# Large attentions: probabilities turned in 32x32 squares and through DRAM scratch, context sums two slots later

## Chip, cores and metric

One Trainium2 chip, one core. The metric is device time in microseconds; the kernel before takes 2303.13 us (median of 3 runs, 2302.65 to 2303.64).

## What is computed

Two decoder layers' worth of cross attention over 8 batches: a first attention with 16 heads of 32 and its MLP, then two attentions with 16 heads of 128 (`a` = 0 and 1), each with one extra key and value row, and a last MLP. The change concerns the two large attentions. Cut to what matters, with h the normalized rows (8 x 112 of them, 512 wide) and ctx the context (8 x 375 keys, 512 wide):

```
for a in (0, 1):
    h = layer_norm(x)
    q = (h @ wq + bq).reshape(8, 112, 16, 128)
    k = concat(ctx @ wk + bk, bias_k)          # 376 keys, 16 heads of 128
    v = concat(ctx @ wv + bv, bias_v)
    weights = softmax(einsum('bqhk,bthk->bhqt', q, k) / sqrt(128))
    x = x + einsum('bhqt,bthk->bqhk', weights, v).reshape(8, 112, 2048) @ wo + bo
h = gelu(layer_norm(x) @ w_fc1 + b_fc1) @ w_fc2 + b_fc2
return x + h
```

## The kernel before

Each product is made of three fp32r matmuls of halves (hi x hi, lo x hi, hi x lo; lines 1766, 1767, 1768), so every operand is split into a hi half (ScalarE) and a lo half (VectorE or GpSimd).

An attention runs over 4 groups of 4 heads, in each over 8 batches b = 0 to 7 (`Place`; two batches are a pair, four a quad, `parity` = b % 2 picks the buffer), in each over 4 tiles t = 0 to 3, one head each. I call one pass of the loop over t in `one_batch` a slot. In a slot TensorE makes the keys of the tile three slots on (`key`, 12 matmuls of 376 columns into ps_k), one column of context sums (`context_sum`, 9 matmuls of 448 columns) of the batch before, turns the probabilities of the next tile (`turn`, line 1963: three transposes against an identity into ps_t), and makes the scores of the tile two slots on (`scores`, 3 matmuls of 376 columns). The value projection is taken out of the sum over keys: a context sum is the context weighted by the probabilities of all four heads (moving operand `pt`, 4 x 112 columns), four of them (d = 0 to 3) per batch; after each quad `head_output` multiplies the sums with the value weights, 12 matmuls of 448 columns for each of 4 heads. `chunks` and `heads` say which sums and outputs lie in which slot: a slot of b = 1 or 5 has outputs in t = 0 and 1 (not in group 0 for b = 1) and two sums in t = 2 and 3.

The softmax of a tile: VectorE takes the maximum (1538), ScalarE the exponential with its sum (1141), VectorE the reciprocal, the extra key's probability and the scaling (1423, 1547, 1426). After the turn ScalarE writes the hi half of the turned tile (1117) and VectorE the lo half (1554). ScalarE and VectorE also split keys (1110, 1532) and sums (1124, 1560). All engines run instructions in program order, and each of the functions named exists once per engine, in the same order of slots. All DMAs are issued by SyncE in program order on one queue; an issue whose semaphore is not there yet holds all that follow. The context comes from DRAM scratch, as halves by feature (`cs`, two buffers) and by key (`ckd`, two buffers of 2 x 768 KB). The value weights of the next group are loaded late in b = 1 (`place.loads`), and their halves made there: hi on ScalarE (899), lo on GpSimd (806).

At the end of an attention (`epilogue`) come the last sums and outputs, then the output projection (`project`), 7 row tiles of 12 matmuls of 512 columns for each of 4 groups; its first two row tiles (`EARLY_TILES`) take operands that lie ready early, the third waits for all output evictions (z_ev), and the halves of its operands are made by ScalarE 1212 and VectorE 1636.

## Time and profile before

| | |
|---|---|
| time, median of 3 runs | 2303.13 us |
| profiled execution: span from first to last instruction | 2301.3 us |
| first large attention, about | 604 to 1220 us of the span |
| second large attention, about | 1390 to 2066 us |
| TensorE busy | 2273.7 us (99%) |
| VectorE / ScalarE / GpSimd busy | 1339.3 / 1122.5 / 359.4 us |
| granted TensorE clock | 0.999 of full speed |
| DMA | 376.25 MB, 163 GB/s on average |

For the profiled execution the profile gives the span; a run's time holds a little more, what lies before the first and after the last instruction (2303.13 - 2301.3 = 1.8 us by the median). In rows with durations, an instruction's start and how long it was in the engine stand first; matmuls are pipelined, so that what one costs is the distance between two starts and not its length. Busy shares are averages over the span.

### The profile page before, as it was taken

The page shows a single profiled execution, that of the slowest core. Times are in us where ns is not written, and L with a number is a line of the kernel's source. Part 1 is how long each engine was busy: PE and PEld are TensorE (multiplying, and loading weights), DVE is VectorE, ACT ScalarE, POOL GpSimd, SP SyncE. Part 2 cuts the span into 40 slices and gives each one's busy share as a digit, 9 for nine tenths or more (in the row PEclk, how much of TensorE's full clock was granted, in tenths as well). Part 3 has the DMA queues.
Part 4 walks back from the last instruction along what each step waited for, and adds up shares of the span by engine and source line. Part 5 has one row for each costly group of instructions (what it writes and reads, how often), then busy time and mean ns, then how long its engine had stood idle before and what let it go on. Part 6 is the DMA issues. An engine that isn't in the chain of part 4 may idle for free.

```text
span 2301.3 us, 37087 instructions
## 1 busy us (share of the span) xinstructions
PE 2273.7 (99%) x13091; PEld 2061.8 (90%) x13091; DVE 1339.3 (58%) x3102; ACT 1122.5 (49%) x2468; POOL 359.4 (16%) x727
## 2 busy tenths in 40 slices
PE   7999999999999999999999999999999999999999
PEld 6777788889999999999998899999999999998887
DVE  6877774524655655665664526565565565564743
ACT  5777753344444445454453434445445445453421
POOL 2111065320000101001002210001001001012421
PEclk9999999999999999999999999999999999999999
DMA  5422135574554755745744554555556556454110
GB/s 196 139 90 104 62 112 195 170 245 134 191 191 151 237 181 166 232 170 181 230 142 146 210 167 147 205 192 184 193 191 198 179 191 213 164 167 132 54 55 33
DMA packets 255224, 376.25 MB, mean 163 GB/s; under 512 B 90302, under 2 KB 205906, under 8 KB 255042
## 3 DMA queue, kind: packets, MB, share of 16 engines
q1 hardware_dynamic: 255042, 373.87, 48.3%
q8 instruction: 108, 1.77, 0.3%
q14 instruction: 74, 0.61, 0.1%
HBM read 315.77 MB, written 58.05 MB: 162 GB/s over the span
## 4 chain that ended last, share of the span: by engine, by line
PE 94%; DVE 3%; ACT 1%; issue 1%; DMA 0%; SPq 0%; DVEq 0%; ACTq 0%
PE ps_k L1766 10%; PE ps_k L1767 10%; PE ps_k L1768 10%; PE ps_o L1766 9%; PE ps_o L1768 9%; PE ps_o L1767 9%; PE ps_v L1766 6%; PE ps_v L1768 6%; PE ps_v L1767 6%; PE ps_s L1766 4%; PE ps_s L1768 4%; PE ps_s L1767 4%; PE ps_t L1963 3%; PE ps_t L1901 2%; PE ps_s L1888 1%
## 5 line engine op out<-in xcount | busy, mean ns | idle before, releaser
L1766 PE MATMUL ps_k<-cs_hi,w_a_hi 128*128 128x376 f32 x1132 | 383.0, 338 | 0.0
L1767 PE MATMUL ps_k<-cs_lo,w_a_hi 128*128 128x376 f32 x1132 | 378.6, 334 | 0.0
L1768 PE MATMUL ps_k<-cs_hi,w_a_lo 128*128 128x376 f32 x1132 | 377.6, 334 | 0.0
L1141 ACT ACTIVATE prob<-ps_s,row_columns 112x376 f32<-112x376 f32 x256 | 147.2, 575 | 304.0 <-DVE row_columns L1538 304.0
L851 POOL CAST k_hi<-xk_hi 128x1 fp32r<-128x1 f32 x256 | 47.0, 184 | 1226.6 <-PE ps_s L1768 1226.6
L1766 PEld LDWEIGHTS ps_k<-cs_hi,w_a_hi 128*128 128x128 f32 x1132 | 213.1, 188 | 1.3 <-issue 0.3
L1767 PEld LDWEIGHTS ps_k<-cs_lo,w_a_hi 128*128 128x128 f32 x1132 | 213.2, 188 | 0.5
L1768 PEld LDWEIGHTS ps_k<-cs_hi,w_a_lo 128*128 128x128 f32 x1132 | 213.2, 188 | 0.0
L1532 DVE SCALAR_TENSOR_TENSOR k_lo<-ps_k,col_b,k_hi 128x375 fp32r<-128x375 f32 x252 | 152.8, 606 | 72.5 <-ACT k_hi L1110 66.9
L1110 ACT ACTIVATE k_hi<-ps_k,col_b 128x375 fp32r<-128x375 f32 x252 | 143.7, 570 | 82.7 <-PE ps_k L1768 81.7
L1423 DVE RECIPROCAL row_columns<-row_columns 112x1 f32<-112x1 f32 x384 | 62.6, 163 | 195.1 <-ACT prob L1141 187.4
L806 POOL TENSOR_TENSOR w_b_lo<-w_raw_b,w_b_hi 128x512 fp32r<-128x512 f32 x80 | 108.0, 1379 | 387.3 <-ACT w_b_hi L899 387.2
L1426 DVE TENSOR_SCALAR prob<-prob,row_columns 112x375 f32<-112x375 f32 x384 | 162.7, 424 | 4.5
L1560 DVE TENSOR_TENSOR sums_lo<-ps_o,sums_hi 128x448 fp32r<-128x448 f32 x128 | 80.0, 625 | 131.2 <-ACT sums_hi L1124 131.1
L1538 DVE TENSOR_REDUCE row_columns<-ps_s 112x1 f32<-112x376 f32 x256 | 138.4, 540 | 8.3 <-PE ps_s L1768 8.1
L1768 PE MATMUL ps_o<-pt_hi,ckd_lo 128*128 128x448 f32 (+1 forms) x384 | 140.6, 366 | 0.0
L1766 PE MATMUL ps_o<-pt_hi,ckd_hi 128*128 128x448 f32 (+1 forms) x384 | 140.5, 366 | 0.0
L1767 PE MATMUL ps_o<-pt_lo,ckd_hi 128*128 128x448 f32 (+1 forms) x384 | 140.0, 365 | 0.0
L1124 ACT ACTIVATE sums_hi<-ps_o 128x448 fp32r<-128x448 f32 x128 | 69.8, 545 | 141.4 <-PE ps_o L1768 141.3
L1768 PE MATMUL ps_v<-pt_hi,ckd_lo 128*128 128x448 f32 x378 | 138.4, 366 | 0.0
L1767 PE MATMUL ps_v<-pt_lo,ckd_hi 128*128 128x448 f32 x378 | 137.6, 364 | 0.0
L1766 PE MATMUL ps_v<-pt_hi,ckd_hi 128*128 128x448 f32 x378 | 137.4, 364 | 0.0
(283 smaller groups left out, 5749.5 us busy)
## 6 DMA issues: line engine op xcount, KB each, us to landing
ckd_hi<-context_by_key_halves SPq DMA_DIRECT2D x64, 768.0 KB, 4.5
ckd_lo<-context_by_key_halves SPq DMA_DIRECT2D x64, 768.0 KB, 6.4
cs_hi<-context_halves SPq DMA_DIRECT2D x64, 752.0 KB, 6.2
cs_lo<-context_halves SPq DMA_DIRECT2D x64, 752.0 KB, 7.9
w_raw_b<-in_blocks_b SPq DMA_DIRECT2D x104, 256.0 KB, 4.1
w_raw_a<-in_blocks_a SPq DMA_DIRECT2D x104, 256.0 KB, 4.3
q<-q_scratch SPq DMA_DIRECT2D x72, 224.0 KB, 6.3
extra<-extra_probability SPq DMA_DIRECT2D x16, 896.0 KB, 5.1
```

Source lines behind the costliest of these rows:

```text
L806: pool.tensor_tensor(w[slot][1][:, :, part], w_raw[slot][:, :, part], w[slot][0][:, :, part], ALU.subtract).then_inc(w_lo[slot], 1)
L1110: act.activation(k[t % 2][0][:, 0:LK], key_bank(place, t)[:, 0:LK], ACT.Identity, bias=col_b[:, ds(place.column((C_BK0, C_BK1), t), 1)]).t ...
L1124: act.activation(sums[0][:, d, place.quarter * HALF:(place.quarter + 1) * HALF], ps_c[d % 2][:, 0:HALF], ACT.Identity).then_inc(c_hi, 1)
L1141: act.activation(prob[buf][0:LQ, 0:KW], ps_s[buf][0:LQ, 0:KW], ACT.Exp, bias=max_neg[0:LQ, buf:buf + 1], accum_out=prob_sum[0:LQ, buf:buf ...
L1426: dve.tensor_scalar(p[0:LQ, 0:LK], p[0:LQ, 0:LK], prob_rcp[0:LQ, col:col + 1], None, ALU.mult).then_inc(s_norm, 1)
L1532: dve.scalar_tensor_tensor(out=k[t % 2][1][:, 0:LK], in0=key_bank(place, t)[:, 0:LK], scalar=col_b[:, ds(place.column((C_BK0, C_BK1), t), 1)],
L1538: dve.tensor_reduce(max_neg[0:LQ, t % 2:t % 2 + 1], ps_s[t % 2][0:LQ, 0:KW], AX_X, ALU.max, negate=True).then_inc(s_max, 1)
L1560: dve.tensor_tensor(sums[1][:, d, cols], ps_c[d % 2][:, 0:HALF], sums[0][:, d, cols], ALU.subtract).then_inc(c_lo, 1)
L1766: pe.matmul(out, w_h, m_h, start=first, stop=False)
L1767: pe.matmul(out, w_h, m_l, start=False, stop=False)
L1768: return pe.matmul(out, w_l, m_h, start=False, stop=last)
L1963: last = pe.transpose(ps_t[buf][0:n, i * LQ:(i + 1) * LQ], prob[buf][0:LQ, k0:k0 + n], ident[0:LQ, 0:LQ])
```

## The change

The probabilities are no longer turned by TensorE. VectorE transposes each tile in 32x32 squares into one buffer, `blocks` (128 x 1536 for the 4 heads of a batch); SyncE stores `blocks` to DRAM scratch and loads it back with 4 DMAs of 32 partitions each, which puts the squares where the turned matrix has them, into the lo half of `pt`; ScalarE makes the hi half of a whole batch in one pass (`turned_hi`, 1536 columns) and GpSimd the lo half in three (`turned_lo`, 512 columns each). The context sums of a batch move two slots later. Queries are padded from 112 to 128 rows per batch in scratch and in the scores (so the query parts are 448 and 448 columns instead of 512 and 384); keys alternate between two PSUM banks; `ckd` becomes one buffer in four parts, each loaded when the sum that used it is done; outputs of a quad lie in t = 2 and 3; weights of the next group are split in t = 0 and 1 of b = 2 and loaded in t = 1 of it. In the epilogue the last two sums of b = 6 and the first two row tiles of the projection lie ahead of the last batch's sums, and the four last outputs are made in two halves.

```diff
-        self.loads = isinstance(self.b, int) and self.b == 1 and not self.head
+        self.loads = isinstance(self.b, int) and self.b == att.loading and (group > 0 or not att.layer and not self.head)
...
-        return {2: (0, 1), 3: (2, 3)}.get(t, ()) if self.att.layer and self.loads else ()
+        return {0: (0, 1), 1: (2, 3)}.get(t, ()) if self.att.layer and self.loads else ()
...
         def chunks(place, t):
 
-            if place.before() is None:
+            last = place.before()
+            if t >= 2:
+                return () if last is None or outputs_here(place) else ((last, t - 2),)
+            if last is None or last.before() is None:
                 return ()
-            if place.final:
-                return {0: (0,), 1: (1, 2), 2: (3,)}.get(t, ())
-            if place.quarter != 1 or place.head:
-                return (t,)
-            return {2: (0, 1), 3: (2, 3)}.get(t, ())
+            return ((last.before(), 2 * t), (last.before(), 2 * t + 1)) if outputs_here(last) else ((last.before(), t + 2),)
...
+                def store_blocks(place):
+                    sp.wait_ge(block_turn, unit_1(place, NT))
+                    sp.sem_inc(sp_waited, 1)
+                    sp.dma_start(turned_scr[place.parity], blocks[:]).then_inc(blocks_out, 16)
+
+                def load_turned(place):
+                    sp.wait_ge(blocks_out, 16 * place.visit + 16)
+                    wait(sp, c_mm, NT * (place.visit - 1))
+                    sp.sem_inc(sp_waited, 1)
+                    src = turned_scr[place.parity].rearrange("(i a) (s f) -> s a i f", i=BANDS, s=4)
+                    for s in range(4):
...
+                        sp.dma_start(dst, src[s]).then_inc(turned_in[place.parity], 16)
...
+                    for t in range(NT):
+                        if t == 0 and place.after(2):
+                            sp.wait_ge(k_mm, place.tile + NT)
...
+                            load_halves(place.after(2))
...
+                        if t == 1 and place.after(2):
+                            load_q(place.after(2))
+                        if t == 2:
+                            store_extra(place)
+                            store_blocks(place)
+                        if t == 3:
+                            load_turned(place)
...
+                        for summed, d in chunks(place, t):
+                            load_by_key(summed.next(), d)
+                        if t == 1 and place.loads:
+                            load_block(1, place.block_b + 1)
+                            load_block(0, place.block_a + 1)
...
+                def turned_lo(place):
+                    pool.wait_ge(t_hi, place.visit + 1)
+                    for i in range(3):
...
+                        pool.tensor_tensor(lo, lo.bitcast(F32), hi, ALU.subtract).then_inc(t_lo, 1)
...
+                        if t == 1 and place.before():
+                            turned_lo(place.before())
                         split_lo(1, place.block_b, place.split_own(t))
...
+                def turned_hi(place):
+                    act.wait_ge(turned_in[place.parity], 64 * place.pairs + 64)
+                    act.activation(pt[place.parity][0][:], pt[place.parity][1][:].bitcast(F32),
+                                   ACT.Identity).then_inc(t_hi, 1)
...
                         if place.key(t + 2):
                             exp(*place.key(t + 2))
+                        if t == 0 and place.before():
+                            turned_hi(place.before())
...
+                    outputs_hi(a, 0, (z_half, a + 1))
                     for t in range(NT):
                         extra_term(place, t)
-                    outputs_hi(a, 0, (z_mm, NT * place.quads + NT))
...
+                    dve.wait_ge(s_norm, place.unit + t + 1)
+                    if t == 0:
+                        wait(dve, blocks_out, 16 * place.visit)
+                    dve.transpose(blocks[:].rearrange("p (s j t e) -> p t j s e", s=4, j=3, t=NT)[:, t],
+                                  prob[buf][:, 0:BLOCKS * SQUARE].rearrange("p (j s e) -> p j s e", j=3, s=4)).then_inc(block_turn, 1)
...
+                    for c in range(len(OUT_CHUNKS)):
+                        outputs_lo(a, 0, c)
                     for t in range(NT):
                         output(place, t)
-                    for c in range(len(OUT_CHUNKS)):
-                        outputs_lo(a, 0, c)
...
                     if d == 0:
-                        pe.wait_ge(t_lo, NT * place.visit + NT)
-                        pe.wait_ge(ck_in[place.parity], 32 * place.pairs + 32)
+                        pe.wait_ge(t_lo, 3 * place.visit + 3)
+                    pe.wait_ge(ck_in[d], 16 * place.visit + 16)
...
                 def epilogue(place):
-                    first_final_sum(place)
-                    for d in range(1, DT):
+                    for d in (2, 3):
+                        context_sum(place.before(), d)
...
+                    for r in range(EARLY_TILES):
+                        project_row(1, 0, 0, 5 * RT + 4 * RT * a, r, early)
+                    for d in range(DT):
                         context_sum(place, d)
-                    for t in range(NT):
-                        head_output(place, t)
+                    for part in ((0, 2), (2, DT)):
+                        for t in range(NT):
+                            head_output(place, t, part)
```

How the order of instructions moves, at three places. A number behind a name is the buffer's.

ScalarE, the end of one batch and the first slot of the next in an ordinary stretch; before:

```order
L1110 ACTIVATE k1_hi<-ps_k,col_b 128x375 [waits k_mm,s_mm]
L1124 ACTIVATE sums_hi<-ps_v 128x448 [waits c_mm]
L1117 ACTIVATE pt0_hi<-ps_t1 128x3x112 [waits t_mm]
L1141 ACTIVATE prob0,row_columns<-ps_s0,row_columns 112x376 [waits t_mm,s_max]
L1110 ACTIVATE k0_hi<-ps_k,col_b 128x375 [waits k_mm,s_mm]
```

and now:

```order
L1178 ACTIVATE k1_hi<-ps_t0,col_b 128x375 [waits k_mm,s_mm]
L1190 ACTIVATE sums_hi<-ps_v 128x448 [waits c_mm]
L1207 ACTIVATE prob0,row_columns<-ps_s0,row_columns 128x376 [waits block_turn,s_max]
L1183 ACTIVATE pt0_hi<-pt0_lo 128x1536 [waits turned_in0]
L1178 ACTIVATE k0_hi<-ps_k,col_b 128x375 [waits k_mm,s_mm]
L1190 ACTIVATE sums_hi<-ps_o1 128x448 [waits c_mm]
```

The hi half of a tile in each slot has become one pass of 1536 columns per batch, behind the exponential (L1207) of slot 0.

GpSimd and SyncE, slots 0 to 2 of b = 2 in groups 1 to 3 (before, the weights w_b lay in b = 1 and GpSimd had no `pt`); now on GpSimd:

```order
L859 TENSOR_TENSOR w_b_lo<-w_raw_b,w_b_hi 128x4x128 [waits w_hi_b] x2
L904 COPY k0_hi<-xk_hi 128x1 [waits s_mm]
L905 COPY k0_lo<-xk_lo 128x1
L912 TENSOR_TENSOR pt1_lo<-pt1_lo,pt1_hi 128x512 [waits t_hi]
L912 TENSOR_TENSOR pt1_lo<-pt1_lo,pt1_hi 128x512 x2
L859 TENSOR_TENSOR w_b_lo<-w_raw_b,w_b_hi 128x4x128 [waits w_hi_b] x2
```

and on SyncE:

```order
L612 DMA cs0_hi<-context_halves 128x1504 [waits k_mm]
L612 DMA cs0_lo<-context_halves 128x1504
L618 DMA ckd<-context_by_key_halves 128x768 [waits c_mm] x2
L658 DMA q<-q_scratch 128x4x128 [waits s_mm]
L618 DMA ckd<-context_by_key_halves 128x768 [waits c_mm] x2
L577 DMA w_raw_b<-in_blocks_b 128x4x128 [waits w_lo_b] x4
L577 DMA w_raw_a<-in_blocks_a 128x4x128 [waits w_lo_a] x4
L702 DMA extra_probability<-extra_p 128x4 [waits extra_ev]
L716 DMA turned_probabilities<-blocks 128x1536 [waits block_turn]
L618 DMA ckd<-context_by_key_halves 128x768 [waits c_mm]
L726 DMA pt0_lo<-turned_probabilities 32x4x384 [waits blocks_out,c_mm]
```

The batch's turned probabilities stand behind two weight passes on GpSimd, and the store of this batch's squares behind eight weight loads on SyncE, two of which wait for the weight passes that stand behind the probabilities.

ScalarE at the end of an attention; before:

```order
L1133 ACTIVATE extra<-extra,col_b,extra_delta 128x448 [waits extra_in,z_ev]
L1133 ACTIVATE extra<-extra,col_b,extra_delta 128x448 [waits z_ev] x3
L1212 ACTIVATE act_t_hi<-cs0_hi 128x4x80 [waits z_mm,p_in0]
L1212 ACTIVATE act_t_hi<-cs0_lo 128x3x4x112 [waits z_mm,p_in1]
L1212 ACTIVATE act_t_hi<-cs1_hi 128x2x4x112 [waits z_mm,p_in2]
```

and now:

```order
L1183 ACTIVATE pt1_hi<-pt1_lo 128x1536 [waits turned_in1]
L1190 ACTIVATE sums_hi<-ps_v 128x448 [waits c_mm]
L1190 ACTIVATE sums_hi<-ps_o1 128x448 [waits c_mm]
L1190 ACTIVATE sums_hi<-ps_v 128x448 [waits c_mm]
L1190 ACTIVATE sums_hi<-ps_o1 128x448 [waits c_mm]
L1273 ACTIVATE act_t_hi<-cs0_hi 128x4x80 [waits z_half,p_in0]
L1273 ACTIVATE act_t_hi<-cs0_lo 128x3x4x112 [waits z_half,p_in1]
L1273 ACTIVATE act_t_hi<-cs1_hi 128x2x4x112 [waits z_half,p_in2]
L1199 ACTIVATE extra<-extra,col_b,extra_delta 128x448 [waits extra_in,z_ev]
L1199 ACTIVATE extra<-extra,col_b,extra_delta 128x448 [waits z_ev] x3
```

The terms of the last four outputs (L1199, before L1133) have moved behind the three operand passes of the projection.

## Rows read from the trace of the kernel before

**Rows 1.** The page: busy us (share of the span) and instructions of each engine.

```profile
PE 2273.7 (99%) x13091; PEld 2061.8 (90%) x13091; DVE 1339.3 (58%) x3102; ACT 1122.5 (49%) x2468; POOL 359.4 (16%) x727
```

**Rows 2.** Timeline of TensorE, one slot: start us, length us, engine, line, operation.

```profile
1019.89 0.36 PE L1768 MATMUL ps_o<-pt_hi,ckd_lo 119*128 119x448 f32 x1
1020.09 0.46 PE L1963 MATMUL ps_t<-ident,prob 112*128 112x112 f32 x3
1020.32 0.41 PE L1766 MATMUL ps_s<-k_hi,q 128*112 128x376 f32 x1
...
1020.91 0.34 PE L1766 MATMUL ps_k<-cs_hi,w_a_hi 128*128 128x376 f32 x1
...
1022.97 0.36 PE L1766 MATMUL ps_v<-pt_hi,ckd_hi 128*128 128x448 f32 x1
...
1024.79 0.46 PE L1963 MATMUL ps_t<-ident,prob 112*128 112x112 f32 x3
```

**Rows 3.** The chain that ended last, this slot: start, share of the chain in us.

```profile
1020.25 0.30 PE ps_t L1963 x3
```

**Rows 4.** Timelines of ScalarE and VectorE in the same slot.

```profile
1022.40 0.58 ACT L1141 ACTIVATE prob<-ps_s,row_columns 112x376 f32<-112x376 f32 x1 [1.22 <-DVE row_columns L1538]
1022.96 0.62 ACT L899 ACTIVATE w_a_hi<-w_raw_a 128x512 fp32r<-128x512 f32 x1
...
1020.87 0.62 DVE L1560 TENSOR_TENSOR sums_lo<-ps_o,sums_hi 128x448 fp32r<-128x448 f32 x1 [0.61 <-ACT sums_hi L1124]
1021.41 0.50 DVE L1554 TENSOR_TENSOR pt_lo<-ps_t,pt_hi 128x336 fp32r<-128x336 f32 x1
1021.82 0.54 DVE L1538 TENSOR_REDUCE row_columns<-ps_s 112x1 f32<-112x376 f32 x1
...
1023.42 0.41 DVE L1426 TENSOR_SCALAR prob<-prob,row_columns 112x375 f32<-112x375 f32 x1
```

**Rows 5.** Groups by line and shape: ScalarE passes of SBUF; count, busy us, mean ns.

```profile
L1212 ACT ACTIVATE act_t_hi<-cs_lo 128x1344 fp32r<-128x1344 f32 x8 | 10.6, 1327 | 24.3 <-PE ps_v L1768 24.3
L1212 ACT ACTIVATE act_t_hi<-cs_hi 128x896 fp32r<-128x896 f32 x8 | 7.6, 952 | 8.8 <-PE ps_o L1768 8.8
```

**Rows 6.** Timelines of GpSimd and VectorE: half passes inside an attention, and behind it.

```profile
913.26 2.58 POOL L806 TENSOR_TENSOR w_b_lo<-w_raw_b,w_b_hi 128x512 fp32r<-128x512 f32 x2 [8.65 <-ACT w_b_hi L899]
...
1223.95 5.92 POOL L806 TENSOR_TENSOR w_b_lo<-w_raw_b,w_b_hi 128x512 fp32r<-128x512 f32 x4 [31.97 <-ACT w_b_hi L899]
...
1224.02 2.19 DVE L1636 TENSOR_TENSOR act_t_lo<-cs_hi,act_t_hi 128x896 fp32r<-128x896 f32 x1
```

**Rows 7.** Timeline of SyncE's DMA issues, weight loads in b = 1.

```profile
917.80 5.12 SPq L541 DMA_DIRECT2D w_raw_b<-in_blocks_b  x4
922.97 3.24 SPq L541 DMA_DIRECT2D w_raw_a<-in_blocks_a  x4
```

**Rows 8.** DMA issues: count, KB each, median us from issue to landing.

```profile
cs_lo<-context_halves SPq DMA_DIRECT2D x64, 752.0 KB, 7.9
...
w_raw_a<-in_blocks_a SPq DMA_DIRECT2D x104, 256.0 KB, 4.3
...
context_by_key_halves<-ckd_hi SPq DMA_DIRECT2D x8, 768.0 KB, 3.3
context_by_key_halves<-ckd_lo SPq DMA_DIRECT2D x8, 768.0 KB, 5.4
```

**Rows 9.** Busy time of the engines in one batch: us; clock, DMA share, GB/s last.

```profile
1000.00:1018.77 18.77, 18.77 (x110) 18.06 (x109) 11.32 (x29) 8.93 (x22) 1.21 (x8) 1.00 0.49 179
```

**Rows 10.** Groups by line and shape: what the last outputs of an attention take.

```profile
L1133 ACT ACTIVATE extra<-extra,col_b,extra_delta 128x448 f32<-128x448 f32 x64 | 75.8, 1185 | 8.2 <-DVE o L1570 8.2
...
L1570 DVE TENSOR_TENSOR o<-ps_s,extra 128x448 f32<-128x448 f32 x4 | 2.5, 626 | 7.3 <-PE ps_s L1768 7.3
...
L1636 DVE TENSOR_TENSOR act_t_lo<-cs_lo,act_t_hi 128x1344 fp32r<-128x1344 f32 x8 | 12.5, 1557 | 4.8 <-ACT act_t_hi L1212 4.8
...
L1636 DVE TENSOR_TENSOR act_t_lo<-cs_hi,act_t_hi 128x896 fp32r<-128x896 f32 x8 | 10.9, 1368 | 1.4 <-ACT act_t_hi L1212 1.3
```

370 lines of the change are left out of this document (162 added, 208 removed).

## The prediction

> **What bounds the kernel now.** I read the page first: TensorE is busy for 2273.7 of 2301.3 us [rows 1], so time leaves only where its stream gets shorter, and comes back wherever it has to wait. Then the timeline of TensorE over one slot of a large attention [rows 2]. From the transposes at 1020.09 to those at 1024.79 a slot takes 4.70 us: 12 key matmuls from 1020.91 to 1022.97 (2.06 us), 9 matmuls of a context sum from there to 1024.79 (1.82 us), and 0.82 us for transposes and scores. Nothing waits. The reader should see that the distance between starts counts, not the lengths. A batch is 4 such slots, 18.77 us [rows 9], with TensorE busy throughout and VectorE for 11.3 us, ScalarE for 8.9 us.
>
> **What is saved.** Transposes to first score matmul take 0.23 us, and the first score matmul behind them runs longer than the others; the chain of waits puts 0.30 us of the slot down to the three transposes [rows 3]. There are 2 x 4 x 8 x 4 = 256 of these groups: 256 x 0.30 = 76.8 us. A slot becomes 4.40 us. Padding the stationary queries to 128 leaves the count of moved columns as it is, and 448 + 448 query columns are as many as 512 + 384: nothing. Scores, maximum, exponential and scaling run on 128 partitions instead of 112 at the same columns: nothing. VectorE's lo half of a tile (0.41 us from its start to the next instruction's [rows 4]) makes room for the squares. I have no row for a transpose on VectorE; the scaling of 375 columns takes 0.41 us and a two-input pass of 896 columns 1.37 us, so 0.59 us by columns for 384 [rows 4, 10]. At either end VectorE has about 12 us of work in a batch of 17.6 us and stays hidden.
>
> **The wait that replaces them.** Where does the first sum of a batch stand, and when is its lo half there? Call S the start of the scores in slot 0. Their position today is the transposes' 1020.09, since those are gone. Behind S TensorE runs 0.51 us of scores, slot 1 (4.40) and the keys of slot 2 (2.06), and at S + 6.97 it wants the sum d = 0 of the batch before, which waits for all three lo passes.
>
> The lo passes hang on that slot's exponential. VectorE starts the sum's lo half at 1020.87 (S + 0.78) and the next instruction at 1021.41 (S + 1.32); that is now the maximum. ScalarE's exponential starts 0.58 us behind the maximum's start and the next ScalarE instruction 0.56 us behind that [rows 4]: `turned_hi` starts at S + 2.46. Its 1536 columns: 896 take 0.95 us and 1344 take 1.33 [rows 5], so 1.49 us; done at S + 3.95. GpSimd takes 1.29 us for a pass of 512 columns inside an attention [rows 6], three take 3.87; with 0.1 us of handing over, S + 7.95. So TensorE waits **1.0 us in an ordinary batch**, against 1.2 us that its four slots save. No semaphore in this chain depends on how early the DMAs land.
>
> Per attention the 20 places where it applies, and one in the epilogue:
>
> - 15 ordinary batches (group 0: b = 2, 3, 4, 7; later b = 0, 3, 4, 7 except the last batch): 15 x 1.0 = 15.0 us. In b = 1 and 5 of later groups (5 alone in group 0) outputs stand in these slots, and in b = 6, with two sums in slots 0 and 1, there is room (S + 8.8): no wait.
> - b = 1 of group 0: slots 0 and 1 hold no sums, so TensorE arrives at S + 5.14 and the chain, with no sum ahead of the maximum, ends near S + 7.3: 2.2 us.
> - b = 2 of groups 1 to 3: two weight passes stand ahead of `turned_lo` on GpSimd. ScalarE makes their hi halves behind `turned_hi`, they end at S + 7.1, the extra key's copies at S + 7.4, the lo passes at S + 11.3; with two sums in slot 1 TensorE arrives at S + 8.8. 3 x 2.5 = 7.5 us.
> - b = 3 behind it. On SyncE the loads of w_b wait for the weights' second pair of passes, which GpSimd does behind the lo passes, to S + 13.9. Today too these loads hold SyncE, 5.12 us, and the four of w_a behind them 0.81 us each [rows 7], but nothing urgent follows. Now the store of b = 2's squares does, ready at S + 10: it is issued near S + 17.8, lands at S + 22 (3.3 us [rows 8] and the loads ahead of it), and VectorE, which must not write `blocks` before, stands at the first square of b = 3 from S + 16.7 on, 5.3 us. Behind it are the keys' lo halves and the next maximum. TensorE first waits 1.0 us for a key; then the exponential ahead of `turned_hi` is late, and at the first sum TensorE waits 3.6 us, of which 1.0 is counted above. 3 x 3.6 = 10.8 us.
> - The last batch has no keys left to cover with: TensorE arrives at S + 2.9 for halves that come at S + 8.0, 5.1 us. Its own halves are asked for after 4 sums (7.3 us) and 2 projection tiles (24 matmuls, 5.5 us) and are about 1.0 us late. 6.1 us.
> - The last four outputs: the projection's third row tile waits for all their evictions. Their terms now stand behind three hi passes on ScalarE (320, 1344 and 896 columns, 2.6 us), their evictions behind three lo passes on VectorE (1.56 and 1.37 us and a short one), and as there is one `term` buffer, each takes 1.19 + 0.63 us in turn [rows 5, 10]. From the moment half the output matmuls are done: lo passes to 4.9, then four evictions to about 11.5 us, while TensorE is through its second half (24 matmuls of 0.20) at 4.9. The two row tiles that cover this today lie earlier now: 6.6 us.
> - Between the second and third output of a quad only the scores are left as cover (0.51 us for an eviction of 0.63 and its handovers): about 0.3 us x 7 = 2.1 us. At the start, slots without sums (2.57 us) run ahead of VectorE's 3.1 us per tile: 1.0 us.
>
> Together 15.0 + 2.2 + 7.5 + 10.8 + 6.1 + 6.6 + 3.1 = 51.3, twice 102.6 us. Change: 102.6 - 76.8 = +25.8. The profiled execution's span is 2301.3 us, so the changed one's 2327; the median of the runs lies 1.8 us above the span, so **2329 us**.
>
> **GpSimd's passes, both ways.** Inside an attention a pass takes 1.29 us; behind it, beside VectorE passes of two SBUF operands, four take 5.92 us, 1.48 each, and VectorE's 896-column pass 2.19 instead of 1.37 us [rows 6, 10]. I take 1.29, since that row lies between the same VectorE instructions; 1.48 is the other end: 3 x 0.19 us at 42 places, +24 us, 2353 us. The Trainium skill (GPSIMD Engine Reference, section Specifications) says that GpSimd and VectorE share the SBUF interface, and contend when VectorE works in a two-port mode or on two SBUF inputs; by that rule the scaling of the probabilities would slow the passes too. The trace agrees behind the attention (1.48 us) and shows none of it inside (1.29 us).
>
> **Scratch.** A batch moves 179 GB/s x 18.77 us = 3.36 MB at 0.49 of the engines' time [rows 9]; the store and loads of 786 KB each raise that to about 0.73. Not the bound, as long as the round trip is in time: squares ready at S1 + 3.9 (S1 in slot 1), store 3.3 us, 1.6 us for four issues, 4.3 us to land [rows 8]: S1 + 13.1, and `turned_hi` could start at S1 + 16.6. The other end, 5.4 and 7.9 us, gives S1 + 18.8, 2.2 us late.
>
> **The rivals.**
>
> *The halves are in time (faster).* One mechanism: if the chain from scores to the last lo pass is shorter than I have it, every one of the 42 waits shrinks. From 0.6 us less the change is even (42 x 0.6 = 25); at 1.0 us less the ordinary batches wait for nothing: 2329 - 42 = 2287, and if VectorE also catches up before b = 3's sum, half of 21.6 us more, 2276 us. For it: three parts of the chain are extrapolated (the 1536 columns, GpSimd on contiguous tiles, the maximum right behind the sum). Against it: each is from a row next to its place, and 0.6 us is 8% of 7.95.
>
> *Scratch comes last (slower still).* If store and loads take the upper rows, `turned_hi` is late by 2.2 us at the 42 places: +92, 2421 us. The point where it starts is 3.5 us more than I have. For it: the loads go to 32 partitions each, which no row shows, and share one queue with 1.5 MB of context. Against: 3.5 us of room, and the context is issued either well before the store or behind the loads.
>
> **Numbers.** Forecast 0.68, in time 0.20, scratch last 0.12. About 0.2% (4.6 us) is what a measurement of this kernel can tell from no change. Of the forecast 0.04 falls within it and 0.03 below (the waits at b = 3 and the end partly hidden), of the first rival 0.03 within: faster 0.20, same 0.07, slower 0.73. The forecast's own range is 2303 to 2356 (GpSimd's upper row and a little); to hold 8 in 10 the range goes down to 2278 and leaves out most of the scratch rival: 2278 to 2356.
>
> **What would show it.** The list of waits of TensorE should show first matmuls of context sums waiting for GpSimd's pt_lo about 42 times: about 77 us in all, 1.0 us in most, 2.5 and 3.6 in b = 2 and 3 of groups 1 to 3, 5.1 in the last batch; and about 6.6 us each before two projection tiles, for VectorE's output. GpSimd passes 1.29 us, `turned_hi` 1.49 us. SyncE should hold a store for some 8 us in each b = 2. A slot without waits should be 4.40 us. If these waits are absent, or TensorE waits for ckd or for other DMAs instead, the prediction is wrong in that step; if `turned_hi` waits for its DMA in ordinary batches, the second rival is right.

## The result, and the profile after

| | before | after |
|---|---|---|
| median of the runs, us | 2303.4 (2302.7 to 2304.1, 4 runs) | 2409.0 (2407.3 to 2412.1, 4 runs) |
| ratio to before | | 1.046, 95% interval 1.0445 to 1.0474 |
| span of the profiled execution, us | 2301.3 | 2409.9 |
| mean granted clock of TensorE | 0.999 | 0.979 |

The changed kernel is 4.6% slower. The prediction was 2329 us, within 2278 to 2356: the sign was right, the gain of the shorter slots was more than eaten by waits and by TensorE at half clock, and the size was wrong by 80 us.

The page of after, busy time of each engine, answers to [rows 1]:

```profile
PE 2258.8 (94%) x12323; PEld 2027.3 (84%) x12323; DVE 1384.3 (57%) x3102; ACT 1116.7 (46%) x2276; POOL 609.1 (25%) x919
```

TensorE issues 768 instructions less, the three transposes of 256 groups, and is yet busy for only 15 us less. It stands still for 151.1 us, against 27.6 before. What it waits for, from the list of waits of TensorE in after (engine, what it writes and line, releaser: us in total, times, longest; "issue" is a wait for nothing that the profile shows):

```profile
PE ps_v L1820 <- POOL pt_lo L912: 63.0, 40, 5.1
PE ps_o L1820 <- DVE o L1632: 20.5, 30, 6.3
PE ps_v L1820 <- issue: 18.5, 2, 9.5
PE ps_s L1820 <- DVE k_lo L1594: 16.0, 10, 3.8
...
PE ps_s L1820 <- DVE q L1481: 4.5, 8, 0.9
```

The first two rows are near what was predicted (77 us for all waits for the lo halves, 17 for the outputs), the keys' 16.0 us were forecast as 6, the queries' not at all. The third row is two waits only, one in each attention, of about 9 us: the first sum, forecast among the lo halves at 2.2 us each. The groups by line and shape in after, for the new operations:

```profile
L912 POOL TENSOR_TENSOR pt_lo<-pt_lo,pt_hi 128x512 fp32r<-128x512 f32 x192 | 245.3, 1307 | 227.2 <-ACT pt_hi L1183 227.2
...
L1616 DVE STREAM_TRANSPOSE blocks<-prob 128x384 f32<-128x384 f32 x256 | 148.1, 579 | 68.4 <-DMA turned_probabilities<-blocks 60.3
...
L1183 ACT ACTIVATE pt_hi<-pt_lo 128x1536 fp32r<-128x1536 f32 x64 | 94.5, 1477 | 13.3 <-DMA pt_lo<-turned_probabilities 13.3
```

Each duration is within 0.02 us of the prediction's (1.29, 0.59, 1.49). And the DMA issues of after (count, KB each, median us to landing), which answer to [rows 8]:

```profile
turned_probabilities<-blocks SPq DMA_DIRECT2D x64, 768.0 KB, 3.8
pt_lo<-turned_probabilities SPq DMA_DIRECT2D x256, 192.0 KB, 4.0
```

**Where the span's 108.6 us come from.** I took the starts of TensorE's instructions through both attentions and compared each distance with its distance where nothing waits. Distances above that behind a wait sum to 140.8 us in after, 3.7 in before: +137.1. A 448-column matmul over 28-column runs takes 0.206 us from start to start instead of 0.2025: 3072 of them, +10.8. The share of the clock that was not granted while TensorE was busy sums to 37.6 us in after, none in before. With the -76.8 that were forecast for the transposes: 137.1 + 10.8 + 37.6 - 76.8 = 108.7. Each term is good to a few us only (it depends on which distances count as a wait), so that the sum comes out within 0.1 is luck. This is where the time lies; it does not say yet what each part would give back.

**The clock.** The windows of after, right behind the first sum's wait and over the 50 us around it (us, busy us and instructions of PE, PEld, DVE, ACT, POOL, then granted clock, DMA share, GB/s):

```profile
575.14:579.30 4.16, 4.16 (x12) 3.77 (x13) 1.77 (x4) 0.43 (x1) 0.27 (x2) 0.50 0.48 193
...
550.00:600.00 50.00, 37.63 (x190) 34.88 (x189) 27.09 (x61) 17.99 (x37) 10.34 (x24) 0.90 0.66 207
```

The timeline of TensorE in the same stretch shows what half the clock (1.2 of 2.4 GHz) does:

```profile
575.14 0.71 PE L1820 MATMUL ps_v<-pt_hi,ckd 128*128 128x448 f32 x1 [9.53 <-issue]
575.65 0.57 PE L1821 MATMUL ps_v<-pt_lo,ckd 128*128 128x448 f32 x1
576.02 0.57 PE L1822 MATMUL ps_v<-pt_hi,ckd 128*128 128x448 f32 x1
...
582.12 0.37 PE L1822 MATMUL ps_o<-pt_hi,ckd 128*128 128x448 f32 x1
582.33 0.37 PE L1820 MATMUL ps_o<-pt_hi,ckd 128*128 128x448 f32 x1
```

A matmul starts every 0.37 us instead of every 0.21. In after the granted clock was 0.50 from 569.5 us, within the wait, to 579.7. In before it stayed at 1.00 through both attentions, and TensorE hardly stood still there (3.7 us).

**The first sum.** Why did it wait 9.7 us and not 2.2? SyncE's DMA issues in b = 0 of group 0, in after:

```profile
553.04 0.36 SPq L716 DMA_DIRECT2D turned_probabilities<-blocks  x1
556.83 0.32 SPq L640 DMA_DIRECT2D q_scratch<-o  x1
562.21 0.55 SPq L577 DMA_DIRECT2D w_raw_b<-in_blocks_b  x1
562.87 1.97 SPq L726 DMA_DIRECT2D pt_lo<-turned_probabilities  x4
```

and ScalarE and GpSimd behind it:

```profile
569.77 1.48 ACT L1183 ACTIVATE pt_hi<-pt_lo 128x1536 fp32r<-128x1536 f32 x1 [5.91 <-DMA pt_lo<-turned_probabilities]
...
571.33 1.26 POOL L912 TENSOR_TENSOR pt_lo<-pt_lo,pt_hi 128x512 fp32r<-128x512 f32 x1 [10.95 <-ACT pt_hi L1183]
```

The squares were in scratch at 558.00 (there VectorE's next one starts), but SyncE issued their loads at 562.87, behind the weights of the last query piece, which wait until VectorE has split the weights they overwrite. In slots 0 and 1 of b = 1 TensorE has no sums to do, so the late issue is passed on whole.

### The profile page after: what moved, and what is told of

Its sections match the earlier page's. It is cut to its first block, busy times and chain, and to the rows that moved or that the text cites. A ratio compares the mean times of both kernels' runs of the same rounds, so it can differ in the third digit from the quotient of the medians.

```text
span 2409.9 us, 36258 instructions
## 1 busy us (share of the span) xinstructions
PE 2258.8 (94%) x12323; PEld 2027.3 (84%) x12323; DVE 1384.3 (57%) x3102; ACT 1116.7 (46%) x2276; POOL 609.1 (25%) x919
## 3 DMA queue, kind: packets, MB, share of 16 engines
q8 instruction: 101, 1.65, 0.3%
## 4 chain that ended last, share of the span: by engine, by line
PE 67%; DVE 10%; POOL 6%; ACT 6%; issue 6%; DMA 4%; SPq 1%; DVEq 0%; ACTq 0%; POOLq 0%
PE ps_o L1820 7%; PE ps_o L1822 6%; PE ps_o L1821 6%; PE ps_v L1820 5%; PE ps_v L1822 5%; PE ps_v L1821 5%; POOL pt_lo L912 5%; PE ps_k L1820 5%; PE ps_k L1821 4%; PE ps_k L1822 4%; PE ps_s L1820 3%; PE ps_s L1822 3%; PE ps_s L1821 3%; DMA turned_probabilities<-blocks 3%; PE ps_t L1821 2%
## 5 line engine op out<-in xcount | busy, mean ns | idle before, releaser
L1207 ACT ACTIVATE prob<-ps_s,row_columns 128x376 f32<-128x376 f32 x256 | 147.1, 575 | 378.0 <-DVE row_columns L1600 377.9
L912 POOL TENSOR_TENSOR pt_lo<-pt_lo,pt_hi 128x512 fp32r<-128x512 f32 x192 | 245.3, 1307 | 227.2 <-ACT pt_hi L1183 227.2
L1820 PE MATMUL ps_v<-pt_hi,ckd 128*128 128x448 f32 (+1 forms) x384 | 155.1, 404 | 81.4 <-POOL pt_lo L912 63.0
L1820 PE MATMUL ps_k<-cs_hi,w_a_hi 128*128 128x376 f32 x636 | 219.5, 345 | 0.0
L1821 PE MATMUL ps_k<-cs_lo,w_a_hi 128*128 128x376 f32 x636 | 214.7, 338 | 0.0
L1822 PE MATMUL ps_k<-cs_hi,w_a_lo 128*128 128x376 f32 x636 | 213.2, 335 | 0.0
L1488 DVE TENSOR_SCALAR prob<-prob,row_columns 128x375 f32<-128x375 f32 (+1 forms) x384 | 177.4, 462 | 4.5
L1821 PE MATMUL ps_t<-cs_lo,w_a_hi 128*128 128x376 f32 x512 | 170.8, 334 | 0.0
L1822 PE MATMUL ps_t<-cs_hi,w_a_lo 128*128 128x376 f32 x512 | 170.4, 333 | 0.0
L1820 PE MATMUL ps_t<-cs_hi,w_a_hi 128*128 128x376 f32 x512 | 170.1, 332 | 0.0
L1822 PE MATMUL ps_v<-pt_hi,ckd 128*128 128x448 f32 (+1 forms) x384 | 150.4, 392 | 0.0
L1822 PE MATMUL ps_o<-pt_hi,ckd 128*128 128x448 f32 (+1 forms) x384 | 142.8, 372 | 0.0
L1820 PE MATMUL ps_o<-pt_hi,ckd 128*128 128x448 f32 (+1 forms) x384 | 142.5, 371 | 0.0
```

The costliest lines, as they stand in the source:

```text
L912: pool.tensor_tensor(lo, lo.bitcast(F32), hi, ALU.subtract).then_inc(t_lo, 1)
L1207: act.activation(prob[buf][:, 0:KW], ps_s[buf][:, 0:KW], ACT.Exp, bias=max_neg[:, buf:buf + 1], accum_out=prob_sum[:, buf:buf + 1]).then_i ...
L1488: dve.tensor_scalar(p[rows, 0:LK], p[rows, 0:LK], prob_rcp[rows, col:col + 1], None, ALU.mult).then_inc(s_norm, 1)
L1820: pe.matmul(out, w_h, m_h, start=first, stop=False)
L1821: pe.matmul(out, w_h, m_l, start=False, stop=False)
L1822: return pe.matmul(out, w_l, m_h, start=False, stop=last)
```

## The experiments

Times are medians, to be read against after's 2409.0 us; each kernel had its own runs of before beside it (2302.8 to 2303.5 us). The first four take one suspect each: ScalarE's order, the weights in b = 2, SyncE's order at the start, and the clock.

### ScalarE's hi pass ahead of the exponential

```diff
+                        if t == 0 and place.before():
+                            turned_hi(place.before())
                         if place.key(t + 2):
                             exp(*place.key(t + 2))
-                        if t == 0 and place.before():
-                            turned_hi(place.before())
```

Expected: 

> ScalarE's hi pass over the landed tiles stands ahead of the exponential of its slot instead of behind it. Theory (the late lo halves come from ScalarE's order): turned_hi starts about 1.6 us earlier (S + 0.8 instead of S + 2.46), the last lo pass ends near S + 6.3 instead of S + 7.95, the ordinary wait of 0.8 us is gone, those of 1.2 to 2.3 us lose about 1.5 and the one of the last batch goes from 5.3 to about 3.7; together about 20 us per attention: 2409 -> 2365 us (2355 to 2375). Rival (GpSimd or the scratch transfers set the moment anyway): the waits stay, the exponential is only later: 2405 to 2415 us.

Measured: 2400.1 us (2397.2 to 2405.9), ratio 1.0416 (1.0399 to 1.0434). The waits for the lo halves fell from 63.0 to 29.2 us, as the theory has it, and the ordinary wait is gone. But those for VectorE grew: keys 16.0 to 24.5, queries 4.5 to 14.6, and the first sum 18.5 to 21.0. Where the squares land late (b = 0 of group 0, b = 3), the hi pass now holds the exponential behind it, and with it VectorE. And `turned_hi`, now earlier, waited for its transfer in 32 batches (61.6 us in all) instead of 6 (13.3 us). The order is a cause of the late halves, and changing it alone is worth 9 us, not 44: neither range holds.

### Weights later in b = 2

```diff
-                        if t == 1 and place.loads:
+                        if t == 3 and place.loads:
                             load_block(1, place.block_b + 1)
                             load_block(0, place.block_a + 1)
...
-                        split_lo(1, place.block_b, place.split_own(t))
+                        split_lo(1, place.block_b, place.split_own(t - 1))
```

(the second load goes with the condition of the first)

Expected: 

> In b = 2 of groups 1 to 3 SyncE's loads of the next weights move from slot 1 to the end of slot 3 and GpSimd's two pairs of weight passes one slot later, behind turned_lo. Theory (SyncE is held by its own weight loads, GpSimd by the weight passes): the waits of b = 2 (2.3 us) fall to the ordinary 0.8, those of b = 3 (2.1 for the keys, 3.3 for the lo halves) to 0 and 0.8, and the stretches at half clock behind them go (some 2 to 3 us each place): 6 places x 8 us: 2409 -> 2360 us (2350 to 2372). Rival (the waits of b = 2 and 3 come from the scratch traffic beside the loads): they stay, 2405 to 2412 us.

Measured: 2386.4 us (2385.9 to 2388.5), ratio 1.0363 (1.0347 to 1.0378). That is 23 us, half of what was expected. The waits of b = 2 and 3 went to 0.8 us or nothing; two new ones came. VectorE and SyncE's issues in b = 3 of this run:

```profile
787.57 0.32 SPq L716 DMA_DIRECT2D turned_probabilities<-blocks  x1
...
796.42 2.12 SPq L726 DMA_DIRECT2D pt_lo<-turned_probabilities  x4
...
796.42 0.58 DVE L1616 STREAM_TRANSPOSE blocks<-prob 128x384 f32<-128x384 f32 x1 [4.41 <-DMA turned_probabilities<-blocks]
```

The store took 8.8 us to land, behind the weights and the context in the one queue; VectorE may not write `blocks` before, stood for 4.4 us, and the sum of the next batch waited 3.3 us. In the six places like it the store took 7.6 to 9.3 us. The other new wait: GpSimd and VectorE in slot 1 of b = 2.

```profile
764.99 2.54 POOL L859 TENSOR_TENSOR w_b_lo<-w_raw_b,w_b_hi 128x512 fp32r<-128x512 f32 x2
...
767.86 2.95 POOL L859 TENSOR_TENSOR w_b_lo<-w_raw_b,w_b_hi 128x512 fp32r<-128x512 f32 x2
...
766.47 1.28 DVE L1488 TENSOR_SCALAR prob<-prob,row_columns 128x375 f32<-128x375 f32 x1
...
768.28 1.39 DVE L1481 TENSOR_TENSOR q<-q 128x512 fp32r<-128x512 f32 x1
```

Scaling took 1.28 instead of 0.41 us, the queries' lo half 1.39 instead of 0.65, each beside a GpSimd pass, and TensorE waited 1.95 us for the queries.

### The squares' loads ahead of the late query piece

```diff
+                        if t == 3:
+                            load_turned(place)
                         if query_piece(place, t):
                             last_query(query, a, skip, query_piece(place, t))
...
-                        if t == 3:
-                            load_turned(place)
-                            if place.quarter == 3:
-                                load_extra(place)
+                        if t == 3 and place.quarter == 3:
+                            load_extra(place)
```

Expected: 

> SyncE issues the loads of the turned squares ahead of the late query piece in slot 3 (in b = 0 of group 0 alone that is a difference of order). Theory (in b = 0 SyncE is held by the last query piece and the weights behind it): the loads are issued 4.9 us earlier (558.0 instead of 562.9), the wait at the first sum falls from 9.7 and 9.1 us to about 4 us each, with less time at half clock behind: 2409 -> 2397 us (2393 to 2400). Rival (the landing of the loads, not their issue, is late): within 2 us of 2409.

Measured: 2393.2 us (2390.1 to 2401.8), ratio 1.0397 (1.0376 to 1.0417): -15.8. The timelines of SyncE and TensorE:

```profile
552.51 0.36 SPq L716 DMA_DIRECT2D turned_probabilities<-blocks  x1
557.50 1.75 SPq L726 DMA_DIRECT2D pt_lo<-turned_probabilities  x4
...
568.95 0.51 PE L1820 MATMUL ps_v<-pt_hi,ckd 128*128 128x448 f32 x1 [3.83 <-issue]
```

The loads go out as soon as the store has landed, and 3.8 us of wait are left. Settled: this place, once in each attention, is worth 16 us, nearly a fifth of the miss. By the starts of TensorE, 12 of them lie at the place itself (5.9 and 6.1 us). Why 3.8 us are left and not the 2.2 that were forecast, no run takes apart.

### TensorE kept busy behind the waits

```diff
+            def busy(n):
+                for _ in range(n):
+                    pe.transpose(ps_t[1][:, 0:P], ident[:], ident[:])
...
                     if d == 0:
+                        busy(fillers(place))
                         pe.wait_ge(t_lo, 3 * place.visit + 3)
```

(and the same ahead of the scores of b = 3, slot 0, and of the third row tile)

Expected: 

> No wait is touched; ahead of TensorE's long waits stand transposes of the identity into an unread bank (100, 22, 34, 54, 18 and 70 of them), in length a little under the wait. Theory (the clock that falls behind a wait costs some 38 us by itself): the waits end at the same times, the granted clock stays at full behind them, and 2409 -> 2378 us (2370 to 2390). Rival (the clock falls anyway or the 38 us are not the clock's): within 3 us of 2409; and where the filler at half clock runs past the end of a wait, above 2409.

Measured: 2404.9 us (2401.9 to 2407.1), ratio 1.044 (1.0425 to 1.0456), at a mean clock of 0.997. That is 4 us, between the theory and the rival. The identity's transposes took 0.108 us each, more than I had counted, and ran past the waits. So once more, shorter:

Expected: 

> As the first filler run, whose transposes took 0.108 us each and so ended up to 1.2 us behind the waits that they should fill: now 83, 17, 27, 44, 15 and 54 of them, 9.0 to 1.6 us. Theory (TensorE at half clock behind the waits has a price, but a part of it is taken from the next wait): the first run saved 7 us with some 13 us of overruns, so 2409 -> 2390 us (2384 to 2397). Rival (the half clock costs nothing in the end, since the next wait takes it all): 2404 to 2411. Rival (all 38 us are the clock's): 2371 to 2377.

Measured: 2400.0 us (2397.2 to 2400.6), ratio 1.0414 (1.0396 to 1.0431), clock 0.997. Again between the ranges. Half clock is left in four stretches, behind waits of 1.8 to 2.7 us, and 6.7 us are lost in them while TensorE is busy, against 37.6 in after; the first of them:

```profile
961.10:964.50 3.40, 3.40 (x13) 3.40 (x12) 2.60 (x8) 1.56 (x4) 0.30 (x2) 0.50 1.03 224
```

So some 31 us of clock were given back, and 9 us of time came of it. Where did the others go? In the first sum TensorE's stretch is shorter by 2 us and stays so. In b = 2 to 3 it is not. VectorE, then TensorE, of the shorter filler, and the same two instructions of after:

```profile
779.76 0.58 DVE L1616 STREAM_TRANSPOSE blocks<-prob 128x384 f32<-128x384 f32 x1 [8.37 <-DMA turned_probabilities<-blocks]
...
776.95 1.80 PE L1999 MATMUL ps_t<-ident 128*128 128x128 f32 x15
...
780.88 0.44 PE L1820 MATMUL ps_s<-k_hi,q 128*128 128x376 f32 x1 [2.12 <-DVE k_lo L1594]
```

```profile
780.66 0.58 DVE L1616 STREAM_TRANSPOSE blocks<-prob 128x384 f32<-128x384 f32 x1 [6.59 <-DMA turned_probabilities<-blocks]
...
781.79 0.44 PE L1820 MATMUL ps_s<-k_hi,q 128*128 128x376 f32 x1 [1.96 <-DVE k_lo L1594]
```

TensorE reaches the place at 776.95 instead of 779.83 (781.79 less its wait of 1.96), 2.9 us earlier, but starts only 0.9 us earlier: VectorE stands 8.4 us for the store instead of 6.6. The store's landing sets the moment. By the distances between starts, waits (79 us) and fillers (716 of 0.108 us, 77) through both attentions are about 157 us against 140 of waits in after: some 17 us of what the clock gave back went into them. So half clock is a price where nothing else is late behind it (2 us at each first sum), and is taken out of the next wait where a transfer is.

### Contiguous columns

This kernel leaves out the reordering of the turned columns: it multiplies others of them, and what it returns is not the attention.

```diff
-            by_band = pt[place.parity][part][:].rearrange("p (i j t e) -> p j i t e", i=BANDS, j=3, t=NT)
-            return by_band[0:KEY_TILES[i][1], i, :, :, 0:BAND]
+            return pt[place.parity][part][0:KEY_TILES[i][1], i * HALF:(i + 1) * HALF]
...
-            return tile.rearrange("p (g t e) -> p t g e", g=4 * BANDS, t=NT)[:, t]
+            return tile[:, t * HALF:(t + 1) * HALF]
```

Expected: 

> The sums and the head outputs read 448 columns in one run instead of 28-column runs with 4 (or 96) skipped between them; the number of matmuls, columns and waits is the same, which columns are multiplied is not (the sums and outputs are of other rows). Theory: a matmul takes 0.2033 us from start to start instead of 0.207, 3072 of them: -11 us, 2409 -> 2398 us (2395 to 2401). Rival (the pitch does not hang on the runs): 2409 within 2 us.

Measured: 2402.5 us (2401.9 to 2404.8), ratio 1.0434 (1.0419 to 1.045): -6.5 us. The starts of one sum in slots without a wait, of this run and of after:

```profile
637.29 0.36 PE L1819 MATMUL ps_o<-pt_hi,ckd 128*128 128x448 f32 x1
...
638.91 0.37 PE L1821 MATMUL ps_o<-pt_hi,ckd 119*128 119x448 f32 x1
```

```profile
637.78 0.37 PE L1820 MATMUL ps_o<-pt_hi,ckd 128*128 128x448 f32 x1
...
639.43 0.37 PE L1822 MATMUL ps_o<-pt_hi,ckd 119*128 119x448 f32 x1
```

Eight steps take 1.62 us here and 1.65 there: 0.2025 and 0.206 us. The runs of 28 columns do cost, in the context sums, 2304 of the 3072. The head outputs, which are the rest, stayed at 0.206 us in the median without them, and why these take longer than in before (0.203) is open. The waits grew by 2.4 us besides; the two are what is missing of 11, and the time is outside the theory's range.

### The end of an attention

```diff
+                    extra_term(place, 0)
                     outputs_hi(a, 0, (z_half, a + 1))
-                    for t in range(NT):
+                    for t in range(1, NT):
                         extra_term(place, t)
...
-                    if group == 0 and r == 2:
-                        pe.wait_ge(z_ev, NT * QUADS * GROUPS * (a + 1))
+                    if group == 0 and r in (2, RT - 1):
+                        pe.wait_ge(z_ev, NT * QUADS * GROUPS * (a + 1) - (NT - 1 if r == 2 else 0))
```

(on VectorE `output(place, 0)` stands behind the first `outputs_lo`, the other three outputs behind all of them)

Expected: 

> At the end of each attention the first output's term stands ahead of ScalarE's three hi passes and its eviction behind the first of VectorE's lo passes; the third row tile waits for that eviction alone, which is what its bank needs, and the last row tile for all four. Theory (the order behind the last sums costs 6.4 us per attention and TensorE's clock behind it): both waits fall under 1 us, 2409 -> 2394 us (2390 to 2398). Rival (the row tiles then wait for their lo halves or for banks instead): 2403 to 2409.

Measured: 2390.6 us in the median of three runs (2388.6, 2390.6, 2401.8; a fourth took 10475 us and is left out), ratio 1.0394 (1.0366 to 1.0422). TensorE's waits for VectorE's `o` fell from 20.5 to 7.1 us, the two of 6.3 are gone. That is 13 us of the 18. The rest is the clock behind these waits, as the theory has it: between the last outputs and the end of the half clock TensorE gains 9.3 and 8.8 us on after, 18 in the two attentions.

### The orders together, and again

The four orders in one kernel. Expected: 

> The edits of order together: hi pass first, weights later, loads of the squares ahead of the late query piece, tail. Theory (the cost of the change is orders, not transfers or engines): the parts add up to about -120 us, since without waits the clock stays up too: 2409 -> 2288 us (2270 to 2305), which would be 0.7% below the kernel before. Rival (behind the first wait the next one comes, scratch landing at turned_hi): 2310 to 2340.

Measured: 2360.0 us (2355.9 to 2364.0), ratio 1.0249 (1.0232 to 1.0266). -49 where -121 was expected; the four alone gave -9, -23, -16 and -18. The time is outside both ranges, but what the rival says is what the trace shows: behind the first wait stands the next. `turned_hi` waited for its transfer in 32 batches, 43.7 us in all, and the waits for the queries' lo halves rose from 4.5 to 20.2 us. Two refinements follow from the traces above. First, the hi pass in three parts, which brings GpSimd forward without holding the exponential:

```diff
-                    act.activation(pt[place.parity][0][:], pt[place.parity][1][:].bitcast(F32),
-                                   ACT.Identity).then_inc(t_hi, 1)
+                    for i in range(3):
+                        part = slice(i * D, (i + 1) * D)
+                        act.activation(pt[place.parity][0][:, part], pt[place.parity][1][:, part].bitcast(F32),
+                                       ACT.Identity).then_inc(t_hi, 1)
...
-                    pool.wait_ge(t_hi, place.visit + 1)
                     for i in range(3):
+                        pool.wait_ge(t_hi, 3 * place.visit + i + 1)
```

Expected: 

> ScalarE makes turned_hi in three passes of 512 columns and GpSimd's first lo pass waits for the first of them only; the order of all engines stays. Theory (the lo halves are late by the length of the chain of exponential, hi and lo): GpSimd starts 1.0 us earlier, the ordinary wait of 0.8 us is gone and the longer ones lose 0.8 to 1.0 us: 42 places: 2409 -> 2373 us (2368 to 2381). Rival (GpSimd's pass now meets VectorE's scaling of the probabilities, which took 1.28 instead of 0.41 us beside a GpSimd pass in the run with the weights later, and the keys' halves become late): 2385 to 2400.

Measured: 2391.2 us (2387.2 to 2393.0), ratio 1.0377 (1.0362 to 1.0393): the rival's range, but not its mechanism, since the scaling kept 0.41 us in all but six places. The ordinary waits are gone, but the queries' waits at the end of a group rose to 1.9 us, and those of b = 2 (2.5 us) and for the keys of b = 3 (1.9 to 4.3) stayed: TensorE came sooner to the next wait. Second, the weights' loads apart, on top of the run with the weights later:

```diff
                         if t == 3 and place.loads:
                             load_block(1, place.block_b + 1)
+                        if t == 3 and place.b == 4 and place.group:
                             load_block(0, place.block_a + 1)
```

Expected: 

> As the run with the weights later (2386 us), and the loads of w_a are issued in b = 4 instead of b = 2, behind those of w_b. There the store of b = 3's squares landed 8.8 us after its issue (787.6 to 796.4) instead of 3.3 to 5, behind 2 MB of weights and 1.5 MB of context in the same queue, VectorE stood 4.4 us for it, and the sum of b = 4 waited 3.3 us. Theory (what stands ahead in the queue makes the store late): the store lands in 5 us, the 3.3 us go to 0.8: 6 places x 2.5 us and the clock behind them: 2364 to 2374 us. Rival (the context's loads alone make it late): 2382 to 2388.

Measured: 2367.7 us (2365.8 to 2370.3), ratio 1.0278 (1.0263 to 1.0294), as the theory had it. SyncE and VectorE at the place where the store took 8.8 us:

```profile
788.66 0.32 SPq L716 DMA_DIRECT2D turned_probabilities<-blocks  x1
...
792.95 1.75 SPq L726 DMA_DIRECT2D pt_lo<-turned_probabilities  x4
...
793.13 0.58 DVE L1617 STREAM_TRANSPOSE blocks<-prob 128x384 f32<-128x384 f32 x1
```

4.3 us now, and VectorE does not stand for it; in the six places like it the store took 4.2 to 5.9 us instead of 7.6 to 9.3. What lies ahead in the queue makes the store late. The lateness has moved rather than gone: behind the loads of w_a, in b = 5, the store takes 6.8 to 9.5 us, where TensorE has outputs to do and waits little. The weights with what they hold are 41 us of the change's price. All of it in one kernel (thirds, weights apart, loads first, end):

Expected: 

> Thirds, weights apart, squares' loads ahead of the late query piece, and the tail in one kernel. Theory: the parts add up: 2409 - 36 - 40 - 14 - 13 = 2306 us (2292 to 2322), about the kernel before. Rival (a wait that goes uncovers the next one on VectorE, as the run of the four orders showed with 2360 instead of 2288): 2325 to 2350.

Measured: 2326.7 us (2322.6 to 2329.5), ratio 1.0098 (1.0083 to 1.0113), clock 0.995: the rival's range, 21 us above the sum of the parts. The last run takes GpSimd's weight passes to slots 2 and 3 of b = 2 and splits the queries ahead of the weight column.

```diff
-                        split_lo(1, place.block_b, place.split_own(t - 1))
+                        split_lo(1, place.block_b, place.split_own(t - 2))
```

(and on ScalarE and VectorE `split_q` stands ahead of the split of the weight column)

Expected: 

> As the run of all again (2326.7 us), in which TensorE still waited 1.32 us for the queries' lo half at the end of each b = 2 and 1.88 at the end of each b = 7, and VectorE's pass over two SBUF tiles took 1.59 or 1.62 instead of 0.65 us where it ran beside a GpSimd pass. Now GpSimd's weight passes stand in slots 2 and 3 of b = 2, and the queries' split ahead of the weight column's on ScalarE and VectorE in slot 1. Theory (GpSimd and VectorE hold each other up over SBUF, and VectorE's lateness is passed on): the query pass takes 0.65 us again in b = 2, its wait goes to about 0.4, the one of b = 7 to about 1.2; 2326.7 -> 2318 us (2313 to 2322). Rival (the passes are long for another reason): the query pass stays at 1.6 and the time at 2324 to 2329.

Measured: 2322.8 us (2320.0 to 2328.2, 5 runs), ratio 1.0077 (1.0064 to 1.0091). The query pass of the two kernels, this one first (duration in ns, lowest, median and highest):

```profile
L1485 DVE TENSOR_TENSOR q<-q x72: 624/650/694, 51.2 to 2039.1; 128x512 fp32r<-128x512 f32 x64, 128x448 fp32r<-128x448 f32 x8
```

```profile
L1485 DVE TENSOR_TENSOR q<-q x72: 625/650/1594, 52.0 to 2043.1; 128x512 fp32r<-128x512 f32 x64, 128x448 fp32r<-128x448 f32 x8
```

None takes 1.6 us any more, and its waits fell from 18.9 to 12.6 us: the mechanism is shown. The time moved by 4 us and lies between the two ranges expected, and the runs of the two kernels overlap, so that no gain is shown. The scaling took 0.95 and 1.52 us in slots 1 and 2 instead: GpSimd's passes met another VectorE pass in their new place. In this kernel, TensorE's waits:

```profile
PE ps_v L1826 <- POOL pt_lo L913: 19.7, 14, 4.3
PE ps_s L1826 <- DVE q L1485: 12.6, 14, 1.1
PE ps_o L1826 <- DVE o L1636: 10.8, 23, 1.1
```

How much of these another order could still take away, no run shows. It is 0.8% slower than the kernel before, and no version that I ran beats that one.

## Why the prediction was wrong

**The saving: right.** A slot without a wait takes 4.44 us, 4.40 was predicted; the 0.04 are mostly the nine matmuls of the sum over runs of 28 columns, about 11 us of starts in all, of which the contiguous run gave 6.5 us of time back. I had costed the new layout at nothing because the count of columns was the same, and had no row for its pitch.

**The waits behind the sums: mostly right.** Predicted and measured, from start to start:

| wait | predicted, us | measured, us |
|---|---|---|
| ordinary batch | 1.0 | 0.82, and 1.3 to 2.0 in b = 7 |
| b = 2 of groups 1 to 3 | 2.5 | 2.3 |
| b = 3 behind it, key and sum | 1.0 and 3.6 | 1.8 to 2.3 and 3.3 to 3.5 (4.0 and 1.8 in one group) |
| last batch | 5.1 | 5.3 |
| the last batch's own halves | 1.0 | 1.2 |
| third row tile | 6.6 | 6.4 |

The chain of exponential, hi, three lo passes was right, and so was SyncE held by its weight loads in b = 2 (764.58 to 773.81, the store at 774.63), which the runs confirmed.

**The wait that was most wrong: b = 1 of group 0.** "So the chain ends near S + 7.3: 2.2 us" measured 9.7 and 9.1 us. The chain was followed from the exponential on, with the sentence that nothing in it depends on how early the DMAs land. In b = 0 that is wrong: SyncE issues one late query piece and its weights ahead of the squares' loads. I had counted SyncE's queue in b = 2 and not here. Price: 14 us of waits, 16 us of time by the run that undid it.

**The largest term, put at nothing without a reason: the clock.** The prediction holds no term for TensorE's clock. Behind the long waits TensorE ran at half clock, and 37.6 us went there while it was busy, of 82.9 that the forecast of the span was short. The filler took away 31 of these and gave 9 us of time. The row of before shows a clock of 1.00 in its batch [rows 9], and I read that as a property of the kernel where it went with its unbroken stream. The part that the filler could not give back is the stretch in b = 2 to 3 where the store's landing sets the pace: there the prediction's sum of the waits was too small as well (4.6 us in b = 3, measured 5.4 to 5.8) as the clock's absent.

**The small ones.** Waits between outputs came to 0.85 us per quad instead of 0.3 (0.39 for the second, 0.46 for the third), +4 us per attention; the queries' lo half at the end of a group, 0.6 us each, was not seen; at the start the slots waited 2.7 us, of which before has 1.0 too, so 1.7 instead of 1.0. Predicted waits 102.6, measured 137.1: +34.5. With the clock's 37.6 and the runs' 10.8 that is 82.9, which is the span's 2409.9 less the 2327 forecast (to the last digit by luck, as said above).

**GpSimd both ways.** The row that I took (1.29 us) was right for most lo passes: 1.307 in the mean, 1.29 in the median. But what that row showed, no sharing inside an attention, did not hold for the new passes. In b = 7 of every group one of them stands beside VectorE's pass over the next weights, and both take longer, in after at the first such place:

```profile
695.33 1.37 DVE L1354 TENSOR_TENSOR w_a_lo<-w_raw_a,w_a_hi 128x512 fp32r<-128x512 f32 x1 [0.54 <-ACT w_a_hi L963]
...
696.12 1.74 POOL L912 TENSOR_TENSOR pt_lo<-pt_lo,pt_hi 128x512 fp32r<-128x512 f32 x1
```

Alone they take 0.65 and 1.29 us. In groups 0 to 2 the sum behind them waited 1.3 to 2.0 us instead of 0.82. In an ordinary batch the third lo pass meets the scaling of slot 1, which took 0.64 us instead of 0.41, and in the weights run GpSimd's weight pass stretched one to 1.28 us. The Trainium skill (GPSIMD Engine Reference, section Specifications) has both engines share their SBUF interface, and the trace agrees.

**The rivals.** The halves are in time: rejected, TensorE waits for them in 40 places and at the two first sums. Scratch comes last: rejected for after, where `turned_hi` waits 13.3 us for its DMA in six places, 11.2 of them in the two at the start. But the room was less than the 3.5 us that I had: outside the batches behind outputs the loads landed 1.7 us ahead of it in the median, and at least 3.5 us ahead in 5 of 50. That is why the hi pass 1.6 us sooner met its transfer in 32 batches. And the upper price of a store was real: 5.9 to 6.5 us for the stores of b = 2 in after, 7.6 to 9.3 for those of b = 3 in the weights run. The rival's time, 2421, was near the result for a reason that it did not have.

## What to carry to other kernels

When a stream that never waited gets its first waits, follow every queue for every place where the new transfer stands, the first batch above all: an in-order issuing engine passes on whatever is ahead, and a median landing time says nothing of the one behind 2 MB. Give the waits a second price, TensorE at half clock behind them, but only where no transfer is late next. And count an order's undoing by running it: four that were worth 66 us alone gave 49 together.

## What the runs showed of the hardware

- TensorE's granted clock fell to 0.50 behind the long waits of the first attention (9.7, 2.3, 3.3, 5.3 and 6.4 us) for 3 to 10 us, and stayed at 1.00 through the ordinary batches with their 0.8 us. Transposes of an identity during the waits, at 0.108 us each, kept it at 1.00 in all but four places, which came behind waits of 1.8 to 2.7 us.
- VectorE turned 128 x 384 in 32 x 32 squares in 0.58 us, beside a GpSimd pass too.
- In the context sums, 448 moving columns in runs of 28 took 0.206 us, in one run of 448 0.2025.
- Beside a GpSimd pass over two SBUF tiles, VectorE took 1.14 to 1.78 us for 512 columns of two SBUF tiles instead of 0.65, and for a scaling of 375 0.64 us in most places and up to 1.52 instead of 0.41; the GpSimd pass took 1.74 us instead of 1.29 where it met such a VectorE pass. VectorE's passes with PSUM among their operands kept their length.
- The same store of 768 KB landed in 3.8 us in the median, and in 7.6 to 9.3 us behind weights and context in the same queue.
